# The loads of x_pair: tile by tile over 128 partitions in place of four tiles over 64

## The reference

```python
e = jnp.stack([tbl_0[ids[:, 0]], ..., tbl_31[ids[:, 31]]], axis=1)      # (512, 32, 16)
# layer i of three, x0 = e, h = e at first:
z = (x0[:, :, None, :] * h[:, None, :, :]).reshape(B, F * G, E)
y = relu(einsum('oc,bce->boe', W[i], z) + b[i])                        # 128 outputs
# layers 0 and 1: y[:, :64] is kept and y[:, 64:] is the next h; layer 2 is kept whole
z = sum(concat(kept, axis=1), axis=2)                                   # (512, 256)
h = concat([z, dense_ctx], axis=1)                                      # (512, 272)
h = relu(h @ W_top1 + b_top1); h = relu(h @ W_top2 + b_top2); y = h @ W_top3
```

## Time and profile before

| | us |
|---|---|
| median of 3 runs | 567.95 (567.9 to 568.61) |
| the profiled execution's own time | 571.28 |
| its span, first to last instruction | 569.1 |
| PE busy | 516.9 (91%) |
| VectorE busy | 372.3 (65%) |
| GpSimd busy | 192.2 (34%) |
| ScalarE busy | 140.7 (25%) |

### The profile page before, as it was taken

How to read it: one execution, slowest core, us unless ns; L and a number is a source line. 1 busy time by engine, 2 the same in 40 slices (tenths; PEclk the granted TensorE clock), 3 DMA queues, 4 the chain that set the end, 5 groups by cost and what they waited for, 6 DMA issues and landing times.

```text
span 569.1 us, 3811 instructions
## 1 busy us (share of the span) xinstructions
PE 516.9 (91%) x1332; PEld 253.2 (44%) x1332; DVE 372.3 (65%) x214; ACT 140.7 (25%) x211; POOL 192.2 (34%) x162
## 2 busy tenths in 40 slices
PE   0242979999999999999999999999999999999998
PEld 0131534545454545454444545454545454444446
DVE  1123468785949494949687695949494959675822
ACT  1102122414132222223141414122222213130304
POOL 5771535243352608070625344351703030300000
PEclk9985989999999999999999999999999999999999
DMA  6668977959596959788795959595969789922000
GB/s 214 154 115 216 233 183 161 251 105 247 120 249 124 250 122 234 160 193 208 158 243 123 249 123 251 123 250 108 253 133 238 156 182 252 207 51 74 9 0 0
DMA packets 46546, 95.62 MB, mean 168 GB/s; under 512 B 24464, under 2 KB 27408, under 8 KB 38080
## 3 DMA queue, kind: packets, MB, share of 16 engines
q1 hardware_dynamic: 40416, 94.16, 71.1%
q0 software_dynamic: 4096, 1.06, 1.5%
q10 hardware_dynamic: 2016, 0.17, 0.3%
HBM read 93.27 MB, written 2.10 MB: 168 GB/s over the span
## 4 chain that ended last, share of the span: by engine, by line
PE 84%; DMA 5%; another core or an unknown queue 3%; issue 2%; DVE 1%; POOL 1%; SPq 1%; ACT 1%; DVEq 0%
PE acc L577 74%; PE acc L588 7%; DMA x_scratch<-x_t 3%; DMA x_rot<-x_scratch 1%; POOL gathered L314 1%; PE acc L598 1%; SPq L265 1%; DVE z L377 1%; PE acc L593 1%; DMA row<-in_row 0%; DMA gathered<-in_table,rows_all 0%; PE acc L650 0%; PE x_bank L560 0%; PE h L650 0%
## 5 line engine op out<-in xcount | busy, mean ns | idle before, releaser
L577 PE MATMUL acc<-z,w_direct 128*128 128x512 f32 x1024 | 447.5, 596 | 22.2 <-DVE z L377 17.3
L577 PEld LDWEIGHTS acc<-z,w_direct 128*128 128x128 f32 x1024 | 194.3, 191 | 261.3 <-issue 245.3
L377 DVE TENSOR_TENSOR z<-h,x_pair 128x2048 f32<-128x2048 f32 (+1 forms) x65 | 144.9, 2250 | 138.3 <-issue 85.6
L331 POOL TENSOR_TENSOR z_low<-z,z_high 128x1024 fp32r<-128x1024 f32 x30 | 70.3, 2365 | 256.2 <-ACT z_high L467 256.2
L314 POOL DMA_INDIRECT gathered<-in_table,rows_all x128 | 121.7, 951 | 40.9 <-issue 35.2
L377 DVE TENSOR_TENSOR z<-h_odd,x_pair 128x2048 f32<-128x2048 f32 x32 | 72.2, 2279 | 7.9 <-ACT h_odd L481 7.9
L377 DVE TENSOR_TENSOR z<-h_even,x_pair 128x2048 f32<-128x2048 f32 x32 | 72.3, 2280 | 0.2 <-issue 0.2
L481 ACT ACTIVATE h<-acc,columns 64x512 f32<-64x512 f32 x32 | 20.8, 652 | 166.4 <-PE acc L588 99.5
L481 ACT ACTIVATE kept<-acc,columns 64x512 f32<-64x512 f32 (+1 forms) x48 | 32.8, 683 | 56.0 <-PE acc L577 55.2
L588 PE MATMUL acc<-z_high,w_high 128*128 128x512 f32 x64 | 27.1, 505 | 11.6 <-DVE z_low L384 11.6
L394 DVE TENSOR_REDUCE sum<-kept 128x32 f32<-128x512 f32 x32 | 32.9, 1029 | 6.6 <-ACT kept L481 6.6
(11 more groups left out here) (108 smaller groups left out, 128.8 us busy)
## 6 DMA issues: line engine op xcount, KB each, us to landing
x_pair<-x_scratch SPq DMA_DIRECT2D x128, 512.0 KB, 15.4
x_rot<-x_scratch SPq DMA_DIRECT2D x64, 256.0 KB
x_rep<-x_scratch SPq DMA_DIRECT2D x16, 256.0 KB
w_direct<-in_W SPq DMA_DIRECT2D x2, 1024.0 KB, 6.5
gathered<-in_table,rows_all POOLq DMA_INDIRECT x128
x_scratch<-x_t SPq DMA_DIRECT2D x32, 64.0 KB
x_pair<-in_W_top SPq DMA_DIRECT2D x2, 512.0 KB, 4.5
z<-in_W SPq DMA_DIRECT2D x1, 576.0 KB, 4.3
```

The source lines that it names most:

```text
L331: nc.gpsimd.tensor_tensor(z_low[:, slot_of(pair)], products_of(pair), z_high[:, slot_of(pair)].bitcast(F32), ALU.subtract).then_inc(low_po ...
L377: nc.vector.tensor_tensor(z[:, step.group % Z_SLOTS, first:end], h[:].unsqueeze(1).to_broadcast([P, end - first, N]), x_pair[:, chunk % 2, ...
L577: op = nc.tensor.matmul(acc[pair.layer][:], w_direct[:, first + i], products_of(pair)[:, i], start=i == 0 and pair is OPENS[pair.layer, pa ...
```

## The change

In load_pair each tile is loaded by one DMA over all 128 partitions. Its source is an access pattern written out by hand: rows t and t + 16 of x_dram[c] (step ROT * N, count 2), each repeated for 64 partitions (step 0, count 64), and 512 contiguous elements. A group takes four DMAs of 256 KB in place of two of 512 KB. All four raise the group's semaphore by 16, so that VectorE waits for 64 per use of the buffer in place of 32.

```diff
--- before.py
+++ after.py
@@ -265,10 +265,10 @@
                     sp.dma_start(x_rot[:, j, :], rotated).then_inc(here[1 + j], 16)
 
             def load_pair(c, k):
-                for a in range(2):
-                    rows = x_dram[c, ROT * a + GROUP * k:ROT * a + GROUP * (k + 1), :]
-                    sp.dma_start(x_pair[HALF * a:HALF * (a + 1), c % 2, GROUP * k:GROUP * (k + 1), :],
-                                 rows.unsqueeze(0).to_broadcast([HALF, GROUP, N])).then_inc(xp_here[c % 2][k], 16)
+                x = x_dram[c]
+                for t in range(GROUP * k, GROUP * (k + 1)):
+                    both = bass.AP(x.tensor, x.offset + t * N, [[ROT * N, 2], [0, HALF], [1, N]])
+                    sp.dma_start(x_pair[:, c % 2, t, :], both).then_inc(xp_here[c % 2][k], 16)
 
             store_x(0)
             load_x0(0)
@@ -368,7 +368,7 @@
             def products(step):
                 chunk, k = step.chunk, step.k
                 if step.layer == 1:
-                    dve.wait_ge(xp_here[chunk % 2][k], 32 * (chunk // 2 + 1))
+                    dve.wait_ge(xp_here[chunk % 2][k], 16 * GROUP * (chunk // 2 + 1))
                 if k == 0:
                     dve.wait_ge(h_ready[step.layer - 1], chunk + 1)
                 h = h1 if step.layer == 1 else h2[chunk % 2]
```

## The result

| | before | after |
|---|---|---|
| median, us | 567.99 | 1503.51 (1502.43 to 1505.24) |
| ratio | | 2.647, 95% interval 2.642 to 2.651 |
| span of the profiled execution, us | 569.1 | 1503.1 |
| PE busy | 516.9 (91%) | 672.6 (45%) |
| transfers: MB, mean GB/s | 95.62, 168 | 95.62, 64 |

A forecast was written before the change was run, and what follows sets the result against it. PE bounded the kernel before; two DMA engines carrying x_pair were to bound the changed one. 22.3 + 16 x 90.7 + 16 x 5.0 + 10 + 56 = 1619 us, plus 2, rounded to 1620; range 1440 to 2000.

The forecast's parts named there:

- (4): How x_pair's transfer is spread: its source's outermost count of 2 puts each DMA on two fixed engines of 16; chance 0.86.
- start, to the first x_pair issue: Time before SP issues the first x_pair load: 22.3 us.
- x_pair, 256 DMAs: x_pair loads on two engines at 23.1 GB/s each: 90.7 us per chunk, 16 chunks.
- x0, store, gathers, 16 chunks: The two engines' sixteenth of the other transfers: 3.5 us for x0, some 1.5 for store and gathers, 5.0 per chunk.
- drained queue at the start: The two engines' queue drains twice at the start, around stores and x0 of early chunks: some 5 us each, together 10.
- end: After the last x_pair landing: remaining steps, top layers, one product, last relu and a slow clock, 56 us.
- (2): SP's queue: 8 more x_pair issues per chunk at 596 ns, 4.8 us, hidden behind PE's 30.57 us.
- the queue of the pair: The two engines' queue stays busy in steady state, with half a chunk of x_pair, 45 us, still queued.
- The packets: Sign on the profile page: packets under 8 KB rise by about 24,600 in either case, which says nothing.
- Sixteen engines: Rival: x_pair runs on all 16 engines at 370 GB/s, only the start gains, 562 us; chance 0.11.
- Rotating pairs: Rival: two engines per x_pair DMA but a different pair each time, 560 to 570 us; chance 0.03.
- Two slow engines: Rival: two fixed engines at 14.1 GB/s, or a queue drained in each chunk, 1900 to 2549 us; chance 0.05.

The follow-up runs named there:

- the form that moves at 369 GB/s: Changed kernel with the x_pair source as 32 rows by 4 repeats, tile by tile in 2 KB runs: 561.25 us, 0.989 of the kernel before.
- 16 x 8: Changed kernel with the x_pair source as 16 rows by 8 repeats instead of 2 by 64, tile by tile: 575.4 us, 0.997 of the kernel before.

## Why the prediction was right

**The step that decided** was (4), the outermost count. It rested on an argument from forms, since no row of before had a count below 16, and the runs with 4, 8 and 16 show it: engines used equal the count. The rule of the Trainium skill named beside it (DMA: Bandwidth & Descriptors, "Why a DMA increments its semaphore by 16 and not by 1") agrees with 51, 100 and 201 GB/s at counts of 2, 4 and 8. Which two engines carry the DMA no view shows.

**The sum, term by term**, against the span of 1503.1 us:

| term | forecast | measured |
|---|---|---|
| start, to the first x_pair issue | 22.3 | 22.1 |
| x_pair, 256 DMAs | 1451 | 1313 (256 x 5.13) |
| x0, store, gathers, 16 chunks | 80 | 96 (15 x 6.42, from 88.5 less 16 x 5.13) |
| drained queue at the start | 10 | 20 (what is left) |
| end | 56 | 51 (1503.1 less the last landing at 1452.1) |

Only 15 chunks' stores and x0 stand behind the first x_pair issue; the forecast had 16. The forecast is 116 us too high. That is the price of the transfer, 138 us too high, less what the small terms give back, so two errors partly cancel: 25.6 GB/s per engine in place of 23.1. I took x_rot's row, and from that row the rate over 16 with other transfers mixed in; the upper end, w_direct's 25.8, was right, and the reason that I gave for choosing (two engines contend less than 16) spoke for that end. The last landing is this row of the chain of waits, the landing after the last issue:

```profile
1433.13 19.00 DMA x_pair<-x_scratch
...
1454.57 12.39 PE acc L577 x24
```

The end's 5 us are mostly the slow clock's: 8 us were allowed for it, and its second row, 24 matmuls in 12.39 us where 24 took 10.30 before, shows 2.1.

The small transfers were under-priced: 6.4 us per chunk for 5.0. With 4 engines, whose x_pair issues stand 2.52 us apart, the same remainder is 47.64 less 16 x 2.52, 7.3 us, so it doesn't shrink with more engines for x_pair. What of it is x0 and what the store's small pieces wasn't measured.

**Steps that failed without costing the forecast.** The issues (2) were to be hidden behind SP's idle 21 us at 0.6 us each; with the queue full each holds SP for 5.09 us, and SP became the chain. It follows from (4), but the text priced it as if (4) had not happened. And I had the queue of the pair hold half a chunk of work; in fact SP is about four DMAs ahead. 20.13 us after the last issue the data land, about four times 5.13:

```profile
588.82 5.09 SPq L271
...
593.96 20.13 DMA x_pair<-x_scratch
```

The queue stays filled all the same (share 0.13 to 0.14 from 614 to 624 us), as forecast.

The packets were misread as well. They were to rise by about 24,600 under 8 KB, whatever the engines. All packets rose by 23,041 (46546 to 69587) and those under 8 KB by 31,232, and the shortfall of 1,536 against 24,576 and 32,768 is the small packets' (24464 to 22928): 128 DMAs at 16 engines before, 256 at 2 now. So the packets did say something: they would have told two engines from sixteen.

**The rivals.** Sixteen engines: didn't happen, but its price can be checked: 562 us forecast, 561.25 measured for the form that moves at 369 GB/s. With 16 x 8, at 277 GB/s, no gain was seen. Rotating pairs: the share of 0.13 whenever x_pair alone moves, with several DMAs handed over, excludes them. Two slow engines: 25.6 GB/s excludes it; an engine that writes 64 partitions alone isn't slow, it is the 16 together that are.

## What to carry to other kernels

Before rewriting a load, write down the outermost count of its access patterns. On the source's side, with 128 partitions on the other, it was the number of DMA engines at 2, 4, 8 and 16, and a broadcast of two rows to two halves makes it 2; a small count on the destination's side, or one that doesn't divide 16, wasn't run. Merging two DMAs into one can so leave 2 of 16 engines to do the work, with the same bytes, partitions and runs. Where a broadcast is wanted, the layout can often be permuted (here the weights took it up) until the outermost count is 32, and then the one DMA was a per cent better than the two. To see how many engines a load uses, read the DMA share while it moves alone, or compare the packets under 512 B.

## What the runs showed of the hardware

One DMA engine moved 25.0 to 25.5 GB/s in runs of 2 KB whether 2, 4 or 8 of them worked, and 26.5 in runs of 8 KB with 2. A count of 16 used all engines and still gave 225 to 238 GB/s in 8 KB runs and 277 in 2 KB runs, where 32 gave 397 and 369: for this destination the fewest rows that fill the engines were not enough. Each DMA left one small packet per engine that carried it. Repeating a source row 64 or 8 times cost next to nothing against reading as many different rows (225 and 225 GB/s, 225 to 238 and 229). An issue on SP's queue took 0.6 us while there was room, and as long as a transfer (5.09 us here) when about four DMAs were outstanding; the store and x0 then waited behind x_pair on SP.
